# Turning the layer's normalised rows on VectorE with transfers that place the blocks, and the last batch's output tiles in four banks of their own

## The reference

```python
xn = layernorm(x)
q, k, v = split(xn @ wqkv)                 # 16 heads of 16; relu on q and k
y = causal_linear_attention(q, k, v)       # num / (q . cumsum(k) + 1e-5)
scores = sigmoid(xn @ Wr)                  # 8 experts
cw = top2_weights(scores + router_bias)    # zeros but for two per row
hid_e = silu(xn @ Wg_e) * (xn @ Wu_e)      # 4 experts with an MLP
ffn = sum_e cw_e * (hid_e @ Wd_e) + (cw_4 + cw_6) * xn + cw_7 * relu(xn)
out = x + y @ wo + ffn + causal_conv4(xn)
```

## Time and profile before

| | |
|---|---|
| median of 3 runs | 1334.68 us (1334.46 to 1334.79) |
| the profiled execution | 1334.1 us |
| its span, first to last instruction | 1332.3 us |
| mean granted TensorE clock | 0.997 |
| busy: PE, DVE, POOL, ACT | 1312.0, 1120.6, 822.7, 737.4 us |
| DMA traffic | 73.73 MB |

### The profile page before, as it was taken

One profiled execution on the slowest core, in us unless ns is written; L12 is line 12 of the kernel. 1 busy time (PEld: TensorE's weight loads), 2 busy tenths in 40 slices (PEclk: granted clock), 3 DMA queues, 4 the chain that ended last, 5 costly groups with the idle time before them and its releaser, 6 DMA issues.

```text
span 1332.3 us, 54753 instructions
## 1 busy us (share of the span) xinstructions
PE 1312.0 (98%) x24384; PEld 1136.9 (85%) x24384; DVE 1120.6 (84%) x2574; ACT 737.4 (55%) x1543; POOL 822.7 (62%) x673
## 2 busy tenths in 40 slices
PE   5999999999999999999999999999999999999998
PEld 4888888888888888888888888888888888888887
DVE  7988889888898888898888988888888889888885
ACT  5645566545556455565555564556645655545561
POOL 2676566675575755666656757556666566575554
PEclk9999999999999999999999999999999999999999
DMA  5011211111211111111111011111111111111110
GB/s 181 30 39 66 66 53 47 35 66 66 66 34 50 51 66 65 50 50 35 66 66 65 35 49 51 66 66 50 50 34 67 66 65 35 35 65 50 51 49 18
DMA packets 46828, 73.73 MB, mean 55 GB/s; under 512 B 6529, under 2 KB 42241, under 8 KB 42497
## 3 DMA queue, kind: packets, MB, share of 16 engines
q1 hardware_dynamic: 45888, 69.23, 15.2%
q10 hardware_dynamic: 704, 1.01, 0.2%
HBM read 53.18 MB, written 17.04 MB: 53 GB/s over the span
## 4 chain that ended last, share of the span: by engine, by line
PE 97%; DVE 1%; POOL 0%; ACT 0%; DMA 0%; issue 0%; POOLq 0%; DVEq 0%
PE ring L303 51%; PE scores L303 17%; PE ring L423 7%; PE ring L439 6%; PE scores L372 5%; PE state_sum L386 4%; PE ring L459 2%; PE scores L312 2%; PE scores L354 2%; DMA x_t<-in_L_attn_x_dram 0%; DVE cT L828 0%; ACT qp L548 0%; DVE sm L807 0%; PE scores L321 0%; POOL hid L687 0%
## 5 line engine op out<-in xcount | busy, mean ns | idle before, releaser
L687 POOL TENSOR_TENSOR hid<-hid,cwb 128x512 f32<-128x512 f32 x128 | 172.0, 1343 | 225.4 <-DVE hid L836 224.7
L828 DVE SCALAR_TENSOR_TENSOR cT<-xT,conv_ws,cT 128x512 f32<-128x512 f32 x192 | 292.3, 1561 | 0.0
L675 POOL TENSOR_TENSOR x_t<-x_t,same 128x1024 f32<-128x1024 f32 x32 | 76.9, 2404 | 242.7 <-ACT same L557 242.7
L814 DVE TENSOR_TENSOR state_bd<-state_sum,tables_s 128x256 f32<-128x256 f32 x248 | 103.7, 418 | 135.9 <-PE state_sum L386 135.8
L578 ACT ACTIVATE sg<-ring 128x512 f32<-128x512 f32 x128 | 76.8, 600 | 251.3 <-PE ring L303 251.3
L303 PE MATMUL ring<-xl,wgu_h 128*128 128x512 f32 x512 | 212.3, 415 | 0.0
L691 POOL TENSOR_TENSOR hl<-hid,hh 128x512 fp32r<-128x512 f32 x128 | 208.4, 1628 | 0.0
L303 PE MATMUL ring<-xh,wgu_l 128*128 128x512 f32 x512 | 203.0, 396 | 0.0
L303 PE MATMUL ring<-xh,wgu_h 128*128 128x512 f32 x512 | 202.2, 395 | 0.0
L511 ACT ACTIVATE yh<-yT 128x256 fp32r<-128x256 f32 x128 | 53.5, 418 | 246.5 <-DVE yT L845 246.5
L807 DVE TENSOR_TENSOR sm<-scores,causal_s 128x512 f32<-128x512 f32 x256 | 158.5, 679 | 21.6 <-PE scores L372 21.6
(11 more groups left out here) (118 smaller groups left out, 3528.1 us busy)
## 6 DMA issues: line engine op xcount, KB each, us to landing
cwb<-cw_rows SPq DMA_DIRECT2D x32, 1024.0 KB, 4.7
x_t<-in_L_attn_x_dram SPq DMA_DIRECT2D x32, 512.0 KB, 4.4
out_dram<-x_t SPq DMA_DIRECT2D x31, 512.0 KB, 2.9
cw_rows<-cwt SPq DMA_DIRECT2D x128, 2.0 KB, 1.4
sm<-in_L_attn_wqkv_dram ACTq DMA_DIRECT2D x2, 384.0 KB, 5.0
sm<-in_L_ffn_Wg_dram SPq DMA_DIRECT2D x2, 256.0 KB, 3.5
sm<-in_L_ffn_Wu_dram SPq DMA_DIRECT2D x2, 256.0 KB, 4.6
cwb<-in_L_ffn_Wd_dram SPq DMA_DIRECT2D x1, 512.0 KB, 5.7
```

The source lines that it names most:

```text
L675: pool.tensor_tensor(xb, xb, same[:, :, :], ALU.add).then_inc(s_base1, 1)
L687: pool.tensor_tensor(hid[:, e, :], hid[:, e, :], cwb[:, e, :], ALU.mult).then_inc(s_hid, 1)
L814: dve.tensor_tensor(state_bd[:, n % 4, :].rearrange("p (g m n) -> p g m n", g=C, m=PPG), ST.unsqueeze(2).to_broadcast([P, C, PPG, BLK]), s ...
L828: ins = dve.scalar_tensor_tensor(out=cT[:, c, :], in0=xT[:, j % 2, c, n:n + BT], scalar=conv_ws[:, c, n:n + 1], in1=cT[:, c, :], op0=ALU.m ...
```

## The change

DVE turns the rows of the batch after next, right behind the router (`turn_x`): four 128x256 block transposes into a buffer `xb_t`, in blocks of 32x32. SP then issues 32 transfers of 32 partitions by four runs of 32 numbers (`place_turned`), which put the blocks in their places in `xT`: eight of them between the router's four and the broadcast, the rest behind it. PE's `turn_xn` is left for batch 0 alone, and with it ACT's copies into `xT`. For that POOL's `normalise` stands ahead of `base`, and the second `low_x` one place later. At the head of PE's part of 30 batches stand 34 waits on a semaphore long since passed (`FILL`). In the last batch the four output tiles get the four score banks, each a whole bank, and are made in step: three experts for all tiles, then convolution and attention, then the fourth expert. The halo of `xT` becomes 32 columns wide, and two small buffers shift addresses.

```diff
+    LEAD = 32
+    QUADS = P // 32
+    FILL = 34
...
+        xb_t = sb("xb_t", [P, C, QUADS, T, BLK])
...
+        def turned_at(s, j, k):
+            return (s * BPS + j + k - 1) * (16 * QUADS * QUADS)
...
         @block.sync
...
+                if turning:
+                    place_turned(s, j, k + 1, 0, range(QUADS // 2))
                 sp.wait_ge(cw_out, at(s, j, 16 * P // BLK, (k + 1) * 16 * P // BLK))
...
+            def place_turned(s, j, k, c, quarters):
+                sp.wait_ge(s_turn, at(s, j, 1, k - 1))
+                for a in quarters:
+                    for q in range(QUADS):
+                        row = xT[q * BLK:(q + 1) * BLK, (j + k) % 2, c, LEAD:LEAD + BT]
+                        sp.dma_start(row.rearrange("p (t a n) -> p t a n", t=T, a=QUADS)[:, :, a, :],
+                                     xb_t[a * BLK:(a + 1) * BLK, c, q, :, :]).then_inc(xT_in[c], 16)
...
                 if left:
-                    spread_cw(s, j, 1)
+                    spread_cw(s, j, 1, left > 1)
+                if left > 1:
+                    place_turned(s, j, 2, 0, range(QUADS // 2, QUADS))
+                    place_turned(s, j, 2, 1, range(QUADS))
...
         @block.tensor
...
+                if k:
+                    pe.wait_ge(s_sm, at(s, j, U * ROWS, U * ROWS))
                 pe.wait_ge(s_xh, at(s, j, C, k * C + C))
...
+                def last_output():
+                    pe.wait_ge(s_sm, at(s, j, U * ROWS, U * ROWS))
+                    for e in range(E - 1):
+                        pe.wait_ge(s_hl, at(s, j, T, e + 1))
+                        for t in range(T):
+                            add_hidden(t, SB[t], e, first=e == 0)
+                    pe.wait_ge(s_conv, at(s, j, HALO, HALO))
+                    for t in range(T):
+                        turn_conv(t, SB[t], first=False)
+                        add_attention(t, SB[t])
+                    pe.wait_ge(s_hl, at(s, j, T, E))
+                    for t in range(T):
+                        add_hidden(t, SB[t], E - 1).then_inc(s_op, 1)
+                if not last and s + j:
+                    for _ in range(FILL):
+                        pe.wait_ge(tables_in, 16)
                 for t in range(T):
                     gate_up(t)
...
-                    if t == 1 and not last:
+                    if s == j == 0 and t == 1:
                         for c in range(C):
-                            turn_xn(s, j, 1, c)
+                            turn_xn(0, 0, 1, c)
...
         @block.scalar
...
+            def high_x(s, j, k, c):
+                p = (j + k) % 2
+                if s + j:
+                    act.wait_ge(xT_in[c], turned_at(s, j, k))
...
         @block.gpsimd
...
                 if not last:
-                    for c in range(C):
-                        low_x(s, j, 1, c)
+                    low_x(s, j, 1, 0)
                 weigh(2)
+                if not last:
+                    low_x(s, j, 1, 1)
...
+                if left > 1:
+                    normalise(s, j, 2)
                 if not last:
                     base(s, j, 1)
-                if left > 1:
-                    normalise(s, j, 2)
...
         @block.vector
...
+            def turn_x(s, j, k):
+                dve.wait_ge(s_xn, at(s, j, 1, k + 1))
+                if s + j:
+                    for c in range(C):
+                        dve.wait_ge(xT_in[c], turned_at(s, j, k - 1))
+                for t in range(T):
+                    ins = dve.transpose(xb_t[:, :, :, t, :], xn[:, (j + k) % 2, t, :]
+                                        .rearrange("p (c q n) -> p c q n", c=C, q=QUADS))
+                ins.then_inc(s_turn, 1)
...
                     router(s, j, 1)
+                    if left > 1:
+                        turn_x(s, j, 2)
                     key_sums(s, j, 1)
                     products(s, j, 1)
...
-                    dve.tensor_tensor(xb, OB[t][:, 0:D], xb, ALU.add).then_inc(s_out, 1)
+                    done = SB[t] if last else OB[t]
+                    dve.tensor_tensor(xb, done[:, 0:D], xb, ALU.add).then_inc(s_out, 1)
```

More of the change, by code:

```diff
@@ L121, in layer_kernel @@
         cT = sb("cT", [P, C, BT])
+        xT_room = sb("xT_room", [P, 8])
+        xT = sb("xT", [P, 2, C, LEAD + BT])
+        xb_t = sb("xb_t", [P, C, QUADS, T, BLK])
         rdT = qks
@@ L174, in layer_kernel @@
         s_xT = sem("s_xT")
+        s_turn = sem("s_turn")
+        xT_in = [sem(f"xT_in{c}") for c in range(C)]
         s_xh = sem("s_xh")
@@ L441, in numerators, with turn_conv, add_attention, add_hidden @@
                     ins.then_inc(s_num, 1)
+                def turn_conv(t, dst, first):
+                    for c in range(C):
+                        mm(dst[:, c * P:(c + 1) * P], cT[:, c, t * P:(t + 1) * P], ident_s[:, :], is_transpose=True,
+                           start=first and c == 0, stop=False, skip_group_check=True)
+                def add_attention(t, dst):
+                    ts = slice(t * P, (t + 1) * P)
+                    pe.wait_ge(s_yl, at(s, j, T, t + 1))
+                    product(dst[:, 0:D], [(yh[:, c, ts], yl[:, c, ts], wo_h[:, c, :], wo_l[:, c, :])
+                                          for c in range(C)], first=False, final=False)
+                def add_hidden(t, dst, e, first=False):
+                    ts = slice(t * P, (t + 1) * P)
+                    return product(dst[:, 0:D], [(hh[:, e, ts], hl[:, e, ts], wd_h[:, e, :], wd_l[:, e, :])],
+                                   first=first, final=e == E - 1)
                 def output(t):
-                    ts = slice(t * P, (t + 1) * P)
                     dst = OB[t]
@@ L447, in output @@
                         pe.wait_ge(s_out, at(s, j, T, T + 1))
-                    elif t == 0 or last:
-                        pe.wait_ge((s_y, s_gu, s_y)[t], at(s, j, T, T))
+                    elif t == 0:
+                        pe.wait_ge(s_y, at(s, j, T, T))
                     else:
                         pe.wait_ge(s_sig, at(s, j, T, T + 2 + t))
-                    late = last and t == 0
-                    def turn_conv():
-                        if t == 0:
-                            pe.wait_ge(s_conv, at(s, j, HALO, HALO))
-                        for c in range(C):
-                            mm(dst[:, c * P:(c + 1) * P], cT[:, c, ts], ident_s[:, :], is_transpose=True,
-                               start=c == 0 and not late, stop=False, skip_group_check=True)
@@ L462, in add_hidden @@
[L462 to L482, removed]
+                    if t == 0:
+                        pe.wait_ge(s_conv, at(s, j, HALO, HALO))
+                    turn_conv(t, dst, first=True)
+                    add_attention(t, dst)
@@ L488, in batch @@
                         scores(s, j, 0, 1)
-                    if t == 1 and not last:
+                    if s == j == 0 and t == 1:
                         for c in range(C):
-                            turn_xn(s, j, 1, c)
-                if not last:
-                    heads(s, j, 1)
+                            turn_xn(0, 0, 1, c)
+                if last:
+                    last_output()
+                    return
+                heads(s, j, 1)
                 for t in range(T):
-                    if t == T - 1 and not last:
+                    if t == T - 1:
                         scores(s, j, 1, 0)
@@ L630, in _ @@
             act.activation(sg[:, 0:1], zeros[:, 0:1], ACT.Sigmoid)
-            act.activation(xT[:, 0, :, 0:HALO], zeros[:, 0:C * HALO].rearrange("p (c h) -> p c h", c=C),
+            act.activation(xT[:, 0, :, LEAD - HALO:LEAD], zeros[:, 0:C * HALO].rearrange("p (c h) -> p c h", c=C),
                            ACT.Copy).then_inc(s_halo, 1)
```

45 lines of the change are left out of this document (26 added, 19 removed).

## The result

The changed kernel takes **1500.88 us** (median of 4 runs, 1498.29 to 1505.15) against 1334.68 before: a ratio of **1.1248**, 95% interval 1.1235 to 1.1262. Its profiled execution took 1500.51 us with a span of 1498.7, so the spans differ by 166.4 us.

A forecast was written before the change was run, and what follows sets the result against it. PE's own work was taken to bound the kernel. 29 batches at 3.9 + 1.2 = 5.1 us give 147.9; with batch 0 (+1.9), batch 30 (-0.85) and the last (-5.1), +143.9 on 1334.1 gives 1478 us, range 1380 to 1505.

The forecast's parts named there:

- DVE's order: DVE, each batch: products start after POOL's first wide add, both are held and end 5.87 us later than before.
- The idle time of PE: PE before output tile 3: idles 4.5 us per batch, waiting for DVE's first output add.
- The clock: PE around its idle time: one half-clock stretch per batch, costing between nothing and 1.45 us, taken as 1.2.
- The scan: DVE's scan beside POOL's first wide add: if it holds the add, 0.37 us later per batch, 11 us in all.
- The transfers: SP's 32 transfers per batch and the broadcast behind eight of them: cost nothing, with some 6 us of margin.
- The price of an issue: SP: 0.43 us for each transfer issue, from four issues that take 1.71 us.
- The rival that everything DVE gains is hidden: Batches: all 30 shorter by 0.85 us and the last by 5.1, giving 1303.5 us; chance 0.02.
- The waits of `FILL`: Head of PE's batches: 34 waits cost nothing, at most 1.7 us per batch less the slack.
- The last batch: PE's output tiles begin in free banks, so two waits and a half-clock stretch go: 5.1 us less.
- The rival with one product caught: DVE's products: only the second waits for POOL's add, +1.85 us a batch, 1384 us or 1419 with clock; chance 0.10.

The follow-up runs named there:

- the 1550 us: Kernel before with eight unused statistics on DVE between router and key sums, POOL's wide adds not made to wait: 1550.11 us.
- Without the collision: Changed kernel with POOL's two wide adds also waiting until the next batch's denominators are done: 1337.83 us, ratio 1.0023.
- behind late transposes: Changed kernel with DVE's four transposes after the products instead of ahead of the key sums, POOL's wide adds unchanged: 1492.17 us.
- 1329.66 us: Changed kernel with POOL's wide adds waiting for the denominators and ACT issuing the last eight transfers of a batch: ratio 0.9962.
- three pairs of kernels without the collision: Kernels with waiting adds, without against with FILL: all transfers on SP 1345.61/1337.83 us, eight on ACT 1334.07/1329.66, half the rows on DVE 1328.40/1318.59.
- measured alone: Kernel before with only the last batch's four output tiles put in the score banks: 1329.31 us, ratio 0.9961.
- 1389.74: Kernel before with five unused statistics (1.75 us) on DVE between router and key sums: 1389.74 us, ratio 1.041; also called the 1390 us.
- 1373.11 us: Half the rows turned on DVE, half on PE, 17 extra waits, POOL's wide adds not waiting for denominators: ratio 1.0306; also called the 1373 us.
- the version at 1318.59 us: Changed kernel with channel half 1 turned on PE, 16 transfers, POOL's wide adds waiting for the denominators, 17 extra waits: ratio 0.9888.
- 18 or 216 us: Kernel before with eight extra DVE statistics: 1352.99 us with POOL's wide adds waiting for the denominators, 1550.11 us without.

## Why the prediction was right, and where its sizes were off

The forecast was 1478 us with a range of 1380 to 1505, and the mechanism behind it held step by step.

- *DVE's order.* The transposes took 1.43 us (1.4 forecast), the products started behind POOL's first wide add (by 0.48 us; 0.37 forecast), both were caught, and they ended 5.45 us after their start (5.60 forecast).
- *The idle time of PE.* Forecast 4.5 us a batch, measured 128.1 / 30 = 4.27.
- *The clock was the mis-sized term.* The step "one stretch costs between nothing [...] and 1.45 [...] so I take 1.2" assumed one stretch at half clock in each batch. Six in ten of the falls lasted twice as long (19 of 31). By the page's first line: PE's busy time rose by 38.0 us although 30 batches x 0.85 = 25.5 us of transposes were taken out, so the same work took 63.5 us longer, 2.2 a batch in 29 batches, against 34.8 us in the sum. This is 28.7 us too little, more than the whole miss of 22.5 us (1500.5 against 1478); the rest of the sum was 6 us too high.
- *The scan.* The sum left out that the scan might hold POOL's add. In this batch the scan had 0.44 us to go when the add started, and the add took 2.62 us instead of 2.40; with eight statistics on DVE (the 1550 us) the mean of that add is 2.71. In seven batches of the changed kernel the scan had only 0.09 to 0.11 us to go, and there the add took its 2.40. So a scan of a kT from SBUF does hold it. By the Trainium skill, page "SBUF — State Buffer", section "Who interferes with whom", a DVE instruction with two SBUF inputs contends with a GpSimd instruction that reads SBUF; the traces agree, for the scan with its column of zeros too. It was worth 0.22 us in this batch, less than the 0.37 that the prediction worked out from it.
- *The transfers.* "Cost nothing" was right for the changed kernel only because the products' wait covered them. The price of an issue was too low: 0.43 us was taken from four small transfers, and the new ones took 0.64 to 0.8 on SP (in the batch above 5.09 us for eight and 17.16 for 24). Without the collision they were the next wait (94.9 us on ACT), and behind late transposes they cost as much as the collision did. The rival that everything DVE gains is hidden (1303.5 us) did not come true even with the collision and the late rows out of the way (1329.66 us): the transposes and the later router together use up what DVE had to spare.
- *The waits of `FILL`.* "Cost nothing" missed their sign: 4 to 10 us of gain in three pairs of kernels without the collision. In the changed kernel itself they were not tried.
- *The last batch.* -5.1 us forecast, -5.2 measured alone.
- *The rival with one product caught* was priced at +1.85 us a batch without and 3.05 with the clock. When it was made (1389.74 and 1373.11 us), it cost 2.1 and 1.9 in each batch that was held: idle times of 1.5 to 1.7 us seldom brought the clock down.

## What to carry to other kernels

Before work is added ahead of an instruction on DVE that reads two tensors from SBUF, look at what POOL does at the new time: a delay of 2.8 us cost 18 or 216 us here, by nothing but the place of two adds on POOL. If POOL's work isn't urgent, let it wait for the end of DVE's instructions: in the version at 1318.59 us no wait of PE comes from it, and it was worth 163 us in the changed kernel. And after a large wait has been removed, read the list again: the transfers that it had covered came next, and behind them what DVE had to spare.

## What the runs showed of the hardware that was not expected

- *A small DVE instruction with a single SBUF tensor is held as well.* `vare`, 128x4, took 160 to 165 ns in all 32 batches before, where it began 0.02 us before POOL's low part ended, or later; with the change it starts in the shadow of a POOL instruction in 23 batches and takes 1275 ns in the median. In the batch above it started 0.04 us after POOL's low part and ended 0.02 us after it. The prediction had taken only two-tensor instructions to be held. The same section of the Trainium skill says that a `tensor_scalar` can enter a mode that uses both ports and then contends, when its operands meet certain conditions; the trace agrees as far as the hold goes, and which mode the instruction ran in no row shows. It decided little here: the router, next on DVE, had its scores, in the batch above, only 0.14 us before it began.
- *Long idle times of PE brought the clock down each time, short ones seldom.* With 4.3 us of idle time it fell to 0.50 once a batch, for 3.41 or 6.83 us. Of 26 idle times of 1.4 to 1.7 us (the 1390 us) five were followed by a fall, of 29 of about 1.5 us (the 1373 us) none; that run has two falls in all, behind other waits, and a mean of 0.998.
- *PE can lose a us in each of eight batches without any releaser*, and 34 or 17 waits long since passed take a part of that away or all of it, as the pairs show; what ends that idle time isn't in the profile.
